# Weighted sums of an attention kernel regrouped: from one step a block to one and a half

## The reference

```python
xn = _layernorm(x, axis=-1)
# attention: q = k = v
q = jnp.einsum('bnhd,hed->bnhe', xh, Wq)
scores = jnp.einsum('bnhe,bmhe->bhnm', q, q) / NORM
res = jnp.einsum('bhnm,bmhe->bnhe', softmax(scores), q)
s = res.reshape(B, N, D) @ Wp.T + bp
# feed-forward: five spiking steps, mean of the spikes
h = jnp.square(jax.nn.relu(jnp.einsum('bsd,fd->bsf', xn, W_fc)))
y = jnp.einsum('bsf,df->bsd', h, W_proj)
g = _silu(spike_mean(y))
return x + s * g
```

## Time and profile before

| | us |
|---|---|
| median of 3 runs (2568.12 to 2570.78) | 2570.59 |
| the profiled execution | 2568.32 |
| its span, first to last instruction | 2566.5 |
| TensorE busy | 2481.9 |
| ScalarE busy | 2062.2 |
| VectorE busy | 1520.2 |
| GpSimd busy | 728.1 |

### The profile page before, as it was taken

One profiled execution on the slowest core, in us unless ns is written; L12 is line 12 of the kernel. 1 busy time (PEld: TensorE's weight loads), 2 busy tenths in 40 slices (PEclk: granted clock), 3 DMA queues, 4 the chain that ended last, 5 costly groups with the idle time before them and its releaser, 6 DMA issues.

```text
span 2566.5 us, 63760 instructions
## 1 busy us (share of the span) xinstructions
PE 2481.9 (97%) x23484; PEld 873.1 (34%) x23484; DVE 1520.2 (59%) x2573; ACT 2062.2 (80%) x2129; POOL 728.1 (28%) x681
## 2 busy tenths in 40 slices
PE   5999999999999999999999999999999999999997
PEld 2333333332333333333332333323333233333333
DVE  5547555476554666546666555755547655466573
ACT  3898887887878888788787888878788787887886
POOL 5123331233312233222332222333123331223420
PEclk8999999999999999999999999999999999999999
DMA  3021120211102011120111202112021110201200
GB/s 122 30 70 33 50 67 18 78 41 43 59 25 79 33 45 57 34 85 18 54 48 38 81 18 72 31 47 70 18 75 44 43 60 20 82 34 43 76 18 27
DMA packets 61487, 127.36 MB, mean 50 GB/s; under 512 B 15873, under 2 KB 17154, under 8 KB 58754
## 3 DMA queue, kind: packets, MB, share of 16 engines
q1 hardware_dynamic: 61186, 123.25, 15.4%
HBM read 89.11 MB, written 34.08 MB: 48 GB/s over the span
## 4 chain that ended last, share of the span: by engine, by line
PE 82%; DVE 12%; issue 4%; SPq 1%; DMA 0%; DVEq 0%; POOL 0%; ACT 0%; POOLq 0%
PE acc L639 34%; PE scores L665 19%; PE aux L565 14%; PE aux L556 9%; PE aux L571 2%; DVE r L939 2%; DVE acc_t L991 2%; DVE cnt L957 2%; PE aux L547 2%; PE aux L613 2%; DVE acc_t L989 1%; DVE h_t L945 1%; DVE acc_t L970 1%; DVE res L1000 1%; SPq L462 1%
## 5 line engine op out<-in xcount | busy, mean ns | idle before, releaser
L829 ACT ACTIVATE e<-scores 128x1024 f32<-128x1024 f32 x2048 | 2022.6, 1022 | 443.4 <-PE scores L665 436.8
L639 PE MATMUL acc<-e,v_ones 128*32 128x512 f32 x8192 | 1098.1, 608 | 2.6 <-DVE acc_t L970 1.8
L665 PE MATMUL scores<-query_stack,key_stack 49*128 49x512 f16 x4096 | 800.4, 385 | 2.9 <-ACT e L829 2.7
L665 PEld LDWEIGHTS scores<-query_stack,key_stack 49*128 49x128 f16 x4096 | 207.5, 93 | 964.0 <-ACT e L829 705.4
L565 PE MATMUL aux<-w_proj,h_t 64*128 64x256 f16 x6144 | 460.3, 269 | 6.1 <-issue 6.1
L556 PE MATMUL aux<-xn_t,w_fc 64*128 64x512 f16 x2976 | 448.5, 377 | 5.8 <-DVE h_t L945 5.0
L565 PEld LDWEIGHTS aux<-w_proj,h_t 64*128 64x128 f16 x6144 | 334.2, 94 | 89.6 <-issue 7.0
L1205 POOL TENSOR_TENSOR r_squared<-r 128x512 f32<-128x512 f32 x256 | 268.2, 1048 | 340.1 <-DVE r L939 319.7
L1208 POOL TENSOR_TENSOR h_t<-r_squared,h_t 128x512 f16<-128x512 f32 x256 | 308.8, 1206 | 39.6 <-POOL r_squared L1205 3.6
L970 DVE STREAM_TRANSPOSE acc_t<-acc 128x512 f32<-128x512 f32 x128 | 91.1, 712 | 346.6 <-PE acc L639 346.6
L639 PEld LDWEIGHTS acc<-e,v_ones 128*32 128x32 f32 x8192 | 162.3, 108 | 354.3 <-issue 293.8
(11 more groups left out here) (74 smaller groups left out, 1048.3 us busy)
## 6 DMA issues: line engine op xcount, KB each, us to landing
key_stack<-q_scratch SPq DMA_DIRECT2D x384, 64.0 KB
query_stack<-q_scratch SPq DMA_DIRECT2D x384, 64.0 KB
x_tok<-x SPq DMA_DIRECT2D x16, 1024.0 KB, 4.9
x_out<-x SPq DMA_DIRECT2D x32, 512.0 KB, 3.6
out<-x_out SPq DMA_DIRECT2D x32, 512.0 KB, 2.7
q_scratch<-q_hi SPq DMA_DIRECT2D x32, 256.0 KB
q_scratch<-q_lo SPq DMA_DIRECT2D x32, 256.0 KB
query_stack<-c_scratch SPq DMA_DIRECT2D x128, 4.0 KB
```

The costliest lines, as they stand in the source:

```text
L639: ins = nc.tensor.matmul(acc[STRIP * n:STRIP * (n + 1), :], v_ones[:, j, G * g + n, :], e[:, tile, n % 2, :], start=j == 0, stop=j == TT - 1)
L665: return nc.tensor.matmul(bank, key_stack[base:base + 49, at, j * P:(j + 1) * P], query_stack[base:base + 49, at, half * HALF:(half + 1) * ...
L829: nc.scalar.activation(e[:, tile % NE, :, :], scores[tile % 2][:, :, :], ACT.Exp, scale=4.0 if exact else SCORE_SCALE).then_inc(s.exp_done, 1)
```

## The change

A unit's 16 tiles are cut into five blocks, of 3, 4, 3, 3 and 3 tiles, and a batch has 40 slots in place of 64. In each block TensorE runs the weighted sums of as many half steps as the block has tiles, 7 half steps behind, then two score tiles, side work, a third score tile; in a block of four, three fifths of the side work's pieces go before the third tile and the rest between it and the fourth. A half step left over at a block's edge is done for half the queries (four matmuls of 256 columns); a whole step within a block stays as it was. `pv_done` counts half steps. In the slot counts of the plan each part of the side work gets about the same share of a batch as before, so that one slot holds what one and a half held; two of the four XT groups move from the second part to the third, banks of XT, Q and C are assigned anew, and the due times on VectorE, GpSimd and ScalarE are rewritten in blocks.

```diff
-LAG = 4
-
-BLOCKS = {i: 1 for i in range(8)}
-
-SHARE = [1] * 8
+LAG = 7
+BLOCKS = {0: 3, 3: 4, 7: 3, 10: 3, 13: 3}
+TURNS = [(2 * TT * unit + at, length) for unit in range(UNITS) for at, length in BLOCKS.items()]
...
-BANK = {FC: [k % KF % 3 for k in range(16)], Y: [1, 2, 1, 2], PROJ: [2, 0, 2, 0], XT: [0, 0, 0, 0], Q: [2, 0, 1, 2], C: [1, 2]}
+BANK = {FC: [k % KF % 3 for k in range(16)], Y: [1, 2, 1, 2], PROJ: [2, 0, 2, 0], XT: [0, 0, 2, 0], Q: [1, 2, 0, 1], C: [2, 0]}
...
-PLAIN = {0: (Q, 0), 1: (Q, 1), 2: (Q, 2), 3: (Q, 3), 5: (C, 0), 6: (C, 1)}
+PLAIN = [(XT, 2), (XT, 3), (Q, 0), (Q, 1), (Q, 2), (Q, 3), (C, 0), (C, 1)]
...
-    return (0, 0, 22, 46, 64) if first else (0, 15, 30, 45, 60) if last else (0, 15, 32, 50, 64)
+    return (0, 0, 12, 29, 40) if first else (0, 9, 18, 27, 36) if last else (0, 9, 20, 30, 40)
...
+                def sums(b, at, upto):
+
+                    while at < upto:
+                        step, low = at // 2, at % 2
+                        high = 2 if at // 2 == (at + 1) // 2 and at + 1 < upto else low + 1
+                        unit, j = step // TT, step % TT
...
+                        pe.wait_ge(s.exp_done, b * 128 + (2 * step + 2))
+                        cols = slice(low * HALF // 2, high * HALF // 2)
+                        for n in range(G):
+                            tile = (2 * step + n // 2) % NE
+                            ins = nc.tensor.matmul(acc[STRIP * n:STRIP * (n + 1), cols], v_ones[:, j, G * g + n, :], e[:, tile, n % 2, cols],
+                                                   start=j == 0 and low == 0, stop=j == TT - 1 and high == 2)
+                        ins.then_inc(s.pv_done, high - low)
+                        at += high - low
...
+                    for (at, length), pieces in zip(TURNS, slots):
+                        if at >= LAG:
+                            sums(b, at - LAG, at - LAG + length)
+                        elif not first:
+                            sums(b - 1, 2 * STEPS + at - LAG, 2 * STEPS + at - LAG + length)
+                        score_tile(b, at)
+                        score_tile(b, at + 1)
+                        early = len(pieces) if length == 3 else len(pieces) * 3 // 5
+                        for piece in pieces[:early]:
+                            side(piece)
+                        score_tile(b, at + 2)
+                        for piece in pieces[early:]:
+                            side(piece)
+                        if length == 4:
+                            score_tile(b, at + 3)
...
                     for unit in range(-1, UNITS - 1):
                         of, which = (b, unit) if unit >= 0 else (b - 1, UNITS - 1)
-                        at = TT * unit + TT + LAG - 1 + 0.42
+                        at = len(BLOCKS) * (unit + 1) + 1.4
...
-                                wait_for = 2.9 if unit == 1 else 0.6
+                                wait_for = {-1: 1.1, 1: 0.8, 3: 3.0, 5: 0.6}[unit]
```

More of the change, by code:

```diff
@@ L138, in slot_starts @@
 def slot_starts(begin, end, lengths):
-    share = [SHARE[i % TT] for i in range(begin, end)]
     at, slot, starts = 0, begin, []
     for n, length in enumerate(lengths):
[L143 to L149, removed]
+        upto = max(slot + 1, begin + round((at + length) / sum(lengths) * (end - begin)))
+        starts += [(at + length * i / (upto - slot), slot + i) for i in range(upto - slot)]
         at, slot = at + length, upto
@@ L154, in plan @@
 def plan(first, last, exact):
-    slots, ends = [[] for _ in range(STEPS)], {}
+    slots, ends = [[] for _ in TURNS], {}
     begins = stretches(first, last)
@@ L190, in plan @@
         if n == 1:
-            whole = [(XT, k, (12 if first else 18) + k) for k in range(4)]
+            whole = [(XT, k, (8 if first else 11) + k) for k in range(2)]
         if n == 2:
             at = [index for start, index in starts for half in range(9) if abs(start - 12 * half) < 1e-6]
-            whole = [(kind, k, at[half]) for half, (kind, k) in PLAIN.items()]
+            whole = [(kind, k, at[half]) for half, (kind, k) in enumerate(PLAIN)]
         for kind, k, slot in whole:
@@ L627, in whole_group @@
                     ins.then_inc(s.pe_done[kind], 1)
[L629 to L641, removed]
+                def sums(b, at, upto):
[3 more added lines that the diff above has]
+                        unit, j = step // TT, step % TT
+                        half, g = unit // NG, unit % NG
+                        if j == 0 and low == 0:
+                            wait(pe, s.acct_set, b * 8 + unit)
+                            if half == 0:
+                                pe.wait_ge(s.vones_set, b * 4 + (g + 1))
+                        pe.wait_ge(s.exp_done, b * 128 + (2 * step + 2))
[6 more added lines that the diff above has]
+                        at += high - low
                 def row_maxima(b):
@@ L820, in body @@
                 def body(b, parity, first, last):
-                    tasks = [(0, 42), (1, 50)]
+                    tasks = [(0, 27), (1, 33)]
                     if not first:
[L823 to L826, removed]
+                        tasks = [(-2, 4), (-1, 17)] + tasks
+                    after = [(k, int(placed(first, last, turn))) for k, turn in tasks]
+                    for turn, (at, length) in enumerate(TURNS):
+                        for tile in range(at, at + length):
                             act.wait_ge(s.scored, b * 128 + (tile + 1))
-                            wait(act, s.pv_done, b * 64 + (i - NE // 2 + 1))
+                            wait(act, s.pv_done, b * 128 + (2 * ((tile - NE) // 2) + 2))
                             nc.scalar.activation(e[:, tile % NE, :, :], scores[tile % 2][:, :, :], ACT.Exp,
                                                  scale=4.0 if exact else SCORE_SCALE).then_inc(s.exp_done, 1)
-                        for k, at in after:
-                            if at == i:
+                        for k, when in after:
+                            if when == turn:
                                 tanh(b - (k < 0), k % 4)
@@ L1189, in place_v @@
                 def place_v(b, g):
-                    wait(pool, s.pv_done, (b - 1) * 64 + (NG + g + 1) * TT)
+                    wait(pool, s.pv_done, (b - 1) * 128 + (NG + g + 1) * 2 * TT)
                     wait_apart(pool, s.xn_set, b * 8 + 8)
```

50 lines of the change are left out of this document (17 added, 33 removed).

## The result

| | before | changed |
|---|---|---|
| median us | 2569.36 | 2524.98 |
| ratio, 95% interval | | 0.9825 (0.981 to 0.984) |
| span of the profiled execution | 2566.5 | 2522.7 |
| a middle batch, mean of 14 | 156.96 | 153.46 |

The account below looks back on a forecast made before the run. TensorE, busy 97%, bounds the kernel, ScalarE close behind. A middle batch: -5.8 + 4.5 + 0.4 - 2.8 = -3.7, 14 of them -52; first +4.6, last +1.2, tail -0.4: -47 from 2570.6, 2524 us, range 2495 to 2552.

Parts of the forecast that it names:

- Switches and sums: TensorE entering and leaving blocks of sums: 0.24 us each, three fewer a unit, -5.8 us a middle batch.
- the lower end of zero to 8.3 us a batch: Weight loads of the 32 half groups a batch: hidden and free at one end, fully visible at the other; zero taken.
- exposed loads: Rival: half groups in the sums pay visibly for their weight loads, at full price 133 us more, 2657; chance 0.13.
- a fixed cost per matmul: Rival: each of 2048 added TensorE matmuls costs 25 ns, giving 2575, no change or just slower; chance 0.05.
- the estimate of 2575: Forecast by the skill page's 60 cycles per matmul, 51 us in all on TensorE; left out of the sum.
- Waits for ScalarE: Third and fourth score tiles of a block wait for exponentials to free two buffers: +4.5 us a middle batch.
- The bounds 1.51 and 2.44: Earliest starts, in us after a block's first score tile, of its third and fourth tiles, set by ScalarE's exponentials.
- a third tile that hardly waits: Rival: ScalarE is ahead more often, so half to all of its waits go, 2447 to 2485; chance 0.10.
- The 0.4 allowed for tanh: ScalarE's four extra tanh a batch, with less slack between blocks: +0.4 us a middle batch.
- the term of 0.8 us: FC 15 in slot 27 waits for the bank q 3 holds, VectorE late by 0.3 to 1.5: +0.8 us.
- the sign to look for: For VectorE: the bank wait at q 3 gone, and one under 1.5 us at FC 15.
- The stall that went: q 3 waiting for VectorE to empty a bank, clock drop behind it: 3.6 us a batch, expected to go.

Follow-up runs that it names:

- the two-step blocks: Kernel before with blocks of two whole steps of sums, then four score tiles with side work among them: 2635.5 us, 1.0256.
- that queue mended: Kernel before with split and turn of the second pair behind q 3's split and first-half threshold passes out of the FC stretch: 2528.6 us, 0.9844.
- the queue mended in both: Changed kernel with three VectorE threshold passes moved behind q 3's split: 2506.3 us; kernel before with split and threshold passes both moved later: 2528.6 us.
- the side work early: Changed kernel with all side work of a four-tile block ahead of its third tile: 2525.6 us, 0.9832.
- half the exponentials: Changed kernel with the exponential from batch 1 on taken over half of each score tile only: 2472.6 us, 0.9624.
- the late thresholds: Kernel before with first-half threshold passes, tanh, gates and one combine moved out of the FC stretch, split left in place: 2574.0 us, 1.0018.

## Why the prediction was right, step by step

*The time:* 2524 was forecast, 2525 measured. The mechanism held: switches saved, most of it paid back as waits for ScalarE, and a stall on VectorE that goes. That the time came within 1 us is partly luck, since the misses below, up to 0.9 us a batch, nearly cancel.

*Switches and sums:* right, 0.24 each, shown by the blocks' starts and by doubling them; half groups cost nothing, the lower end of zero to 8.3 us a batch, which the prediction took. The rivals of exposed loads (1.43 becoming 1.5 to 1.7) and of a fixed cost per matmul fall with the block of 1.42; the estimate of 2575, which added the 60 cycles of the Trainium skill (TensorEngine Tiling (Array Packing), § Instruction Overhead) to each matmul, isn't borne out here.

*Waits for ScalarE:* 4.66 a batch measured by taking them away, 4.5 forecast. The bounds 1.51 and 2.44, read from a stretch without side work, held to 0.01 us with it in the changed kernel; in the two-step blocks they came 0.07 later. The rival of a third tile that hardly waits falls. The 0.4 allowed for tanh wasn't needed: blocks with a tanh are as long as those without.

*VectorE:* the place was right (FC 15 in slot 27, behind q 3 and the threshold passes), the size wrong: **the term of 0.8 us measured 1.69**. The prediction had 14.7 us of passes against 14.45 of TensorE and took the middle of 0.3 and 1.5. TensorE's side was right (14.5 by the starts), but the 22 passes from q 1 to q 3 take 16.1 with no wait between them, in each of the 14 batches: the three threshold passes together run 2.54, one of the four of split and turn 1.53, and one of the two small ones behind the transposition 0.96. So even the upper end, 1.5, which was also the sign to look for, was a little short. The stall that went was 3.4 on the mean of 14 batches; 3.6 was read in one (whose steps 38 and 39 are 3.8 above their work).

*What made up for it:* about 0.6 us in three steps of the kernel before (steps 3, 8 and 11, 0.04, 0.53 and 0.08 above their work), which the sum had left standing, is gone after. It and the 0.4 for tanh that wasn't needed make up for the 0.9 that FC 15 waits longer. Middle batch: -5.8 + 4.66 - 3.4 + 1.69 - 0.6 = -3.45, measured -3.50; forecast -3.7.

*First and last batch:* from the start of the kernel to batch 1's first sums 200.00 against 195.46: +4.5, forecast +4.6. From batch 15's to the end 174.25 against 173.62: +0.6, forecast +1.2 - 0.4.

```profile
200.00 1.50 PE L639 MATMUL acc<-e,v_ones 128*32 128x256 f32 x16
...
2348.45 1.50 PE L639 MATMUL acc<-e,v_ones 128*32 128x256 f32 x16
```

*Where the gain came from:* of the 3.5 us of a middle batch the regrouping is worth 1.1 by itself (-5.8 and +4.66), VectorE's queue 1.7 (-3.4 and +1.69), about half, and the rest is the 0.6 just named. The kernel before with that queue mended is as fast, within 0.2%, as the changed kernel: 0.9844 against 0.9825. With the queue mended in both, the regrouped kernel is at 2506.3 for 2528.6, and at 2491.4 with the side work ahead too. Not tried alone: whether the changed kernel lost the stall at q 3 by its due times, by its new bank numbers or by q groups that stand further apart.

## What to carry to other kernels

Before grouping work to save switches, write down when the consumer frees the buffer of the tile after next: two buffers and a pass of 0.93 us gave bounds that took back four fifths of what the switches saved, and they could be read from a stretch where nothing else ran. A wait for a bank behind an in-order engine is a sum of passes: if the due time of one task is moved and too little goes, the wait can turn up at the next bank, and a test that shows no gain says little until the traces are compared. A regrouped kernel comes with new due times; try those alone on the old one, to see which of the two made the gain.

## What the runs showed of the hardware

A wait of TensorE for a bank can cost more than its length, and whether it does was not steady. In the changed kernel FC 15 starts 1.69 us late in each of 14 middle batches and the granted clock stays at 1.00 behind it (windows: stretch, us, busy us of each engine, granted clock, DMA):

```profile
1074.90:1077.00 2.10, 2.10 (x16) 0.60 (x15) 1.29 (x3) 0.15 (x1) 1.68 (x3) 1.00 0.17 21
```

With the side work early it starts 2.13 us late, and in 3 of 14 batches the slot is 7.84 to 7.89 long in place of 6.25; one of those, and a stretch without such a wait:

```profile
915.60:923.50 7.90, 6.11 (x42) 1.54 (x43) 5.35 (x9) 3.74 (x4) 3.81 (x4) 0.78 0.15 35
450.00:458.00 8.00, 7.69 (x65) 2.12 (x61) 7.72 (x12) 6.49 (x8) 3.99 (x4) 1.00 0.01 2
```

A mean of 0.78 over the stretch means part of it at the 1.2 GHz level. With half the exponentials the start was 2.54 late, and 6 of 14 batches lost another 1.4 to 1.6. The kernel before paid this at q 3 in 10 of its 14 middle batches (steps 38 and 39 together 8.97 to 9.10 us long there, 7.51 in the other four, 3.05 and 2.19 without a wait); with the late thresholds the same step lost it in 3 of 14, and step 38 is 5.32 in the others of both kernels. So a drop cost 1.4 to 1.6 us on top of the wait, and waits of one length drew it in some batches and not in others. What decides in which batches it falls stays open.
